# GpSimd adds the two key chunks of the exponentials, and the denominators' products read the sum

## What is computed

```python
sim = jnp.einsum('bhid,bhjd->bhij', q, k) * SCALE
sim = jnp.where(mask[:, None, None, :], sim, max_neg)
sim = jnp.clip(sim, -5.0, 5.0)
attn = jax.nn.softmax(sim, axis=-1)
out = jnp.einsum('bhij,bhjd->bhid', attn, v)
```

## Time and profile before

| | |
|---|---|
| median of 3 runs | 1505.66 us |
| the profiled execution, its time | 1504.98 us |
| its span in the trace | 1503.1 us |
| a turn, for c = 1 to 13 | 68.80 us each |
| PE busy | 1384.4 us, 92% |
| DVE busy | 1077.7 us, 72% |
| ACT busy | 736.7 us, 49% |
| POOL busy | 728.4 us, 48% |

### The profile page before, as it was taken

How to read it: one execution, slowest core, us unless ns; L and a number is a source line. 1 busy time by engine, 2 the same in 40 slices (tenths; PEclk the granted TensorE clock), 3 DMA queues, 4 the chain that set the end, 5 groups by cost and what they waited for, 6 DMA issues and landing times.

```text
span 1503.1 us, 25372 instructions
## 1 busy us (share of the span) xinstructions
PE 1384.4 (92%) x9840; PEld 1009.9 (67%) x9840; DVE 1077.7 (72%) x1626; ACT 736.7 (49%) x1381; POOL 728.4 (48%) x1010
## 2 busy tenths in 40 slices
PE   6986859999999999999999999999999988568998
PEld 2631648586877778686868777786868667356765
DVE  2110899978888888879788888888797862037567
ACT  2213435555555564646555555646465532315455
POOL 4400223747465564656474655656565753530225
PEclk9988889999999999999999999999999999879999
DMA  7316211213121212222131212122221311152313
GB/s 267 117 57 199 60 46 53 65 53 96 46 71 50 68 50 71 65 67 70 51 96 48 70 50 68 50 73 65 64 60 55 82 36 31 35 192 87 114 61 124
DMA packets 66759, 115.82 MB, mean 77 GB/s; under 512 B 10576, under 2 KB 44240, under 8 KB 66512
## 3 DMA queue, kind: packets, MB, share of 16 engines
q1 hardware_dynamic: 49200, 63.69, 14.7%
q0 software_dynamic: 14848, 41.96, 9.4%
q10 hardware_dynamic: 2592, 8.56, 1.7%
HBM read 103.42 MB, written 10.75 MB: 76 GB/s over the span
## 4 chain that ended last, share of the span: by engine, by line
PE 80%; DVE 13%; DMA 3%; issue 2%; POOL 1%; ACT 1%; SPq 1%; POOLq 0%; DVEq 0%; ACTq 0%
PE proj_bank L355 38%; PE score_bank L355 28%; PE sim_bank L355 10%; DVE cand_idx L948 3%; DVE cand_val L947 3%; DVE x_sum L971 2%; PE score_bank L641 2%; DMA comp_stage<-in_comp 1%; PE sim_bank L641 1%; DVE dispatchedT L1085 1%; PE sim_bank L575 1%; POOL exp L1170 1%; POOL v_rows L1141 0%; PE sim_bank L465 0%; DMA x_pair<-x_scratch 0%
## 5 line engine op out<-in xcount | busy, mean ns | idle before, releaser
L1141 POOL DMA_INDIRECT v_rows<-in_V,top_idx x256 | 248.2, 970 | 299.8 <-DVE top_idx L961 217.6
L727 ACT COPY score_row<-score_bank 128x512 f32<-128x512 f32 x512 | 298.5, 588 | 175.5 <-PE score_bank L355 103.0
L947 DVE MAX8 cand_val<-score_row 128x8 f32<-128x2048 f32 x128 | 292.2, 2282 | 103.7 <-ACT score_row L727 103.7
L1170 POOL TENSOR_SCALAR exp<-exp,exp_bound 128x256 f32<-128x256 f32 x512 | 246.9, 499 | 143.4 <-ACT exp L739 142.7
L948 DVE FIND_INDEX8 cand_idx<-cand_val,score_row 128x8 uint32<-128x2048 f32 x128 | 292.5, 2285 | 0.0
L355 PE MATMUL score_bank<-keysT_hi,qT_hi 128*128 128x512 f32 x512 | 219.5, 429 | 26.0 <-ACT score_row L727 25.0
L355 PE MATMUL score_bank<-keysT_lo,qT_hi 128*128 128x512 f32 x512 | 205.5, 401 | 0.0
L355 PE MATMUL score_bank<-keysT_hi,qT_lo 128*128 128x512 f32 x512 | 205.4, 401 | 0.0
L739 ACT ACTIVATE exp<-sim_bank 128x512 f32<-128x512 f32 x256 | 139.0, 595 | 113.8 <-PE sim_bank L355 113.8
L355 PE MATMUL sim_bank<-qT_heads,kT 64*128 64x256 f32 x1024 | 145.8, 403 | 7.7 <-ACT exp L739 7.7
L971 DVE SCALAR_TENSOR_TENSOR x_sum<-v_rows,top_weight,x_sum 128x256 f32<-128x256 f32 x256 | 134.7, 526 | 13.4 <-DMA v_rows<-in_V,top_idx 4.3
(11 more groups left out here) (168 smaller groups left out, 2301.3 us busy)
## 6 DMA issues: line engine op xcount, KB each, us to landing
kT<-den_scratch SPq DMA_DIRECT2D x64, 256.0 KB, 4.0
comp_stage<-in_comp SPq DMA_DIRECT2D x32, 256.0 KB, 3.7
x_pair<-x_scratch SPq DMA_DIRECT2D x32, 256.0 KB, 2.8
f_quads<-in_f POOLq DMA_DIRECT2D x32, 256.0 KB, 5.2
stage<-in_KmT ACTq DMA_DIRECT2D x8, 512.0 KB, 4.5
xT_all_<-in_xT SPq DMA_DIRECT2D x4, 1024.0 KB, 9.8
xT_in<-in_xT SPq DMA_DIRECT2D x16, 256.0 KB, 3.7
x_sum<-in_x SPq DMA_DIRECT2D x32, 128.0 KB, 2.1
```

The source lines that it names most:

```text
L727: nc.scalar.copy(srow[n // PER % 2][:, i * CB:(i + 1) * CB], scb[n % 3]).then_inc(sem("score_evac"), 1)
L947: own(nc.vector.max(cv[:, tile, cs], srow[g % 2][:, :]))
L1141: pool.indirect_dma_start(out=vg[:, k, :], out_offset=None, in_=V_rows, in_offset=bass.IndirectOffsetOnAxis(ap=i8[:, tile, k:k + 1], axis=0))\
L1170: last = nc.gpsimd.tensor_scalar(ex[i % NEX][:, k, :], ex[i % NEX][:, k, :], ub[:, k, c:c + 1], E_LO, ALU.min, ALU.max)
```

## The change

POOL gets a third task in the head loop. After every second head it waits for its own clips (`clip_done`) and for the denominators' products that read the four slots of a new buffer `es` last (`den_full`), and adds the two key chunks of two heads in one instruction of 128x512. PE's denominators read `es`, with one matmul for each head where there were two, after a wait for `exp_summed`. The six exponential buffers become one tensor, so that one instruction can address two of them. The gathers and the subtraction L1179 move: six gathers stand ahead of the heads, one after head 1, one after head 3, and L1179 after head 7 instead of head 5.

```diff
-        ex = [sb(work, f"exp{i}", [P, KT, S]) for i in range(NEX)]
+        exs = sb(work, "exp", [P, NEX, KT, S])
+        ex = [exs[:, i] for i in range(NEX)]
+        es = sb(work, "exp_sum", [P, 4, S])
@@ PE, values(c, j)
-                for k in range(KT):
-                    for q in range(4):
-                        last = mm(den[32 * q:32 * q + 32, :], sel[:, j % 2, :], ex[(H * c + 4 * j + q) % NEX][:, k, :],
-                                  start=(j % 2 == 0 and k == 0), stop=(j % 2 == 1 and k == KT - 1))
+                need(pe, "exp_summed", NP * c + 2 * j + 2)
+                for q in range(4):
+                    last = mm(den[32 * q:32 * q + 32, :], sel[:, j % 2, :], es[:, q, :], start=(j % 2 == 0), stop=(j % 2 == 1))
                 last.then_inc(sem("den_full"), 1)
@@ POOL, the turn
-                    gather(m, 1, range(0, 5))
+                    gather(m, 1, range(0, 6))
@@
+                    if cross and h % 2 == 1:
+                        need(pool, "clip_done", H * c + h + 1)
+                        need(pool, "den_full", 4 * c + h // 4)
+                        i = H * c + h - 1
+                        nc.gpsimd.tensor_tensor(es[:, i % 4:i % 4 + 2, :], exs[:, i % NEX:i % NEX + 2, 0, :],
+                                                exs[:, i % NEX:i % NEX + 2, 1, :], ALU.add).then_inc(sem("exp_summed"), 1)
                     if mid and h == 1:
-                        gather(m, 1, (5,))
+                        gather(m, 1, (6,))
                     if mid and h == 3:
-                        gather(m, 1, (6, 7))
-                    if mid and h == 5:
+                        gather(m, 1, (7,))
+                    if mid and h == 7:
                         need(pool, "ctx_hi", m + 1)
```

## The result

The changed kernel takes 1561.45 us, the median of 4 runs (1560.66 to 1561.72). The kernel before took 1505.41 us beside it (median of 4). The ratio is 1.0382, with a 95% interval of 1.0359 to 1.0404: slower by 56 us, where 1518.7 us was predicted and 1541 was the end of the range.

The account below looks back on a forecast made before the run. It took the bound to pass from PE to the round of POOL and DVE, 0.8 us more a turn: 10.4 + 1.0 + 2.8 - 0.5 = 13.7 us on 1504.98, 1518.7 us. Own range 1511 to 1529; 8 in 10, 1486 to 1541.

Parts of the forecast that it names:

- What bounds the kernel now: Turns 1 to 13: PE is the bound, busy all or nearly all of 68.80 us each.
- What goes from PE: PE's denominators: each group of 16 instructions becomes eight, saving 0.50 us, 2.0 us a turn; PE alone would need 66.8.
- What comes to POOL: POOL's head loop: eight adds a turn at 1.26 us plus a 0.08 us gap each, 10.7 us together.
- Is there room on POOL?: POOL's slack in its round with DVE is 11.0 us a turn against 10.7 added, so the round would need 68.5.
- the round of POOL and DVE: top_idx, gathers, heads, next gathers, L1191, L1156 on POOL, then DVE's value_sum, candidates, merge, top_idx; 69.6 us with collisions.
- a second path: From PE's last group over DVE's last candidates, L971, gathers and heads to the end of the last group: 67.5 us.
- What collides: POOL and DVE slow each other: 1.4 us more, minus 0.7 at the second L1156, plus 0.4 at L1147; round 69.6.
- The clock: PE's waits could let its granted clock fall, as in turn 14; counted at nothing, since a turn's waits come singly.
- The starved case: Rival, 0.20: POOL running without gaps keeps DVE from its turn; value_sum 2.6 us late, round 71.4, 1544 us.
- PE keeps its gain: Rival, 0.25: PE keeps most of its gain, the round being 67.5 to 66.8 us; 1490 us, or 1481.
- the wash: Rival, 0.14: collisions of POOL and DVE stay at 1.0 us, round 68.5 to 68.7 us, 1506 us.
- The other turns: Outside turns 1 to 13: turn 0 adds 1.0 us, turn 14 adds 2.8, turn 15 gives -0.5.

Follow-up runs that it names:

- PE's part alone with its path cleared: Changed kernel without POOL's adds or the wait for them (half of each denominator left out), first reciprocal ahead of the fifth candidates: 1476.24 us, ratio 0.9837.
- the run with the short bias: Changed kernel with the first reciprocal ahead of the fifth candidates and POOL's two bias additions (L1157) cut from 128x256 to 128x1: 1511.51 us, ratio 1.0063.
- the kernel with adds alone: Changed kernel with POOL's adds and PE's wait for them, but the old eight products of two chunks on PE: 1555.42 us, ratio 1.0333.

## Why the prediction was wrong, point by point

**What bounds the kernel now.** Right: PE, 68.8 us a turn, and PE's part alone with its path cleared gave 67.09.

**What goes from PE.** 0.43 us a group and not 0.50. PE's own turn is 67.1, not 66.8. Small.

**What comes to POOL.** Right: adds of 1.29 us on average, each with a gap of 0.1, against 1.26 and 0.08.

**Is there room on POOL?** Near in size, for a kernel that isn't this one. With the reciprocal out of the way the full change has turns of 69.2 us, where I had 69.6, and 1515 us, where I had 1519. The nearness is in part luck: I had a closed round of POOL and DVE setting the whole turn, and the run with the short bias shows that only some 0.4 us of a turn go around it.

**The step that failed** is the list of paths, and with it the sentence that the bound passes from PE to the round of POOL and DVE. It passed to DVE's queue up to the first reciprocal, for which PE waited 2.7 us in most turns. I counted the round through POOL and a second path, from PE's last group over DVE's last candidates, and never looked at `need(pe, "rden_done", ...)` ahead of the group. The path runs from the score row for DVE's third candidates, which PE's Q stage sets, through DVE's queue without a gap, to the reciprocal and to values(2). In the kernel before it had 0.4 us to spare. Its reciprocal ended at 629.41 + 1.74 = 631.15, and the group started at 631.53; the row of DVE's timeline, which I had not put beside the other:

```profile
629.41 1.74 DVE L995 RECIPROCAL den_recip<-score_bank 128x256 f32<-128x256 f32 x1
```

The kernel before had even shown the wait once, in turn 0, behind the long L982 of the earlier trace rows:

```profile
287.50 1.07 PE L355 MATMUL score_bank<-exp,head_selector 128*32 128x256 f32 x16 [1.95 <-DVE den_recip L995]
```

Everything that stretched DVE was costed as if DVE had slack, since it is busy 72%.

**What collides** was sized well for POOL and wrongly for DVE. I had the eight L971 at 7.6 us; they took 7.40. But I charged this only to L1147 on POOL (0.4 us) and let DVE's own queue absorb the 2.8 us. They came out at PE: with a start that was 0.4 us later, the reciprocal ended 3.2 us later in the turn, 0.4 of which had been spare, and the third group started 2.9 us later.

**The moved subtraction** was costed at nothing, since the round holds the same instructions. It is worth 28 us in the changed kernel by where it stands.

**The clock** was counted at nothing, because I expected a turn's waits to come singly. It fell in all thirteen turns, behind a wait of 2.0 to 2.7 us that mostly had one of 0.8 us just ahead of it, and cost 1.5 us each and 2.8 in every third.

**The rivals.** The starved case had the right neighbour, DVE stretched by POOL, and gave 1544 us by way of L1147; POOL waited 1.23 us there and not 2.6. "PE keeps its gain" and the wash are refuted for the full change. That a halved group is not half is true by 0.07 us.

**The other turns** added 4.6 us where I had 3.3: turn 0 1.8 (I had 1.0), turn 14 2.5 (2.8), and turn 15, up to the end of its last group, 0.3 (-0.5).

**The signs and the sums.** The signs that I named came for the most part: groups at 0.57 us, adds at 1.29, L971 at 7.40, and POOL's wait for ACT's exponentials, over the whole run, down from 142.7 to 19.5 us. They price the change on each engine and do not say which wait ends last. Two slips bear on nothing here: 13 x -1.3 + 2.8 - 0.5 is -14.6, and 0.6 us a turn to either side of 1518.7 gives 1511 to 1527, not 1529.

## What to carry to other kernels

Before work is given to an engine with idle time, look for what else shares its operands' way: here the adds were affordable on POOL and were paid by DVE, in the one stretch where DVE had 0.4 us to spare. For each group of instructions that shrinks or comes earlier, list all of its waits with the distance between the release and the start; the smallest is the gain that can be had. And when a helper's work has to be placed beside another engine's, move single instructions (a reciprocal ahead of a search, a subtraction by two heads) before giving up the idea: with the reciprocal early, the subtraction where it had stood and half of the adds it was worth 8 us; as it stood the change cost 56.

## What the runs showed of the hardware that I had not expected

The same wait of PE, 2.2 us, in turns of one run, was followed by a lower granted clock in some and not in others. With 2.0 to 2.7 us it fell in all thirteen turns of the changed kernel, where in most turns a wait of 0.8 us for POOL had ended 1.1 us earlier, and in three of thirteen of the kernel with adds alone, which mostly had no other wait. With half of the adds and the late reciprocal, ten turns had a single wait of 1.7 us, and it fell in none. What decides it was not resolved. A fall cost 1.5 us, in some turns 2.8. POOL memsets of 0.95 us do not slow DVE instructions with two SBUF operands, and a POOL add does, from 0.48 to 1.38 us. A single TENSOR_SCALAR of DVE, 0.4 us elsewhere, took 2.02 us beside the subtraction and three clips of POOL, once in each turn.
